# FFN of layer 0: who normalises the rows, and where VectorE takes x's block maxima and scales

## What is computed

```python
xn = _layernorm(x, axis=-1)                 # (x - mean) / sqrt(var + 1e-5)

def fp4_quant_dequant(x):                   # blocks of 16 along the last dim
    xb = x.reshape(shape[:-1] + (shape[-1] // 16, 16))
    scale = max(max(abs(xb)) / 6, 1e-12)
    xn = xb / scale
    idx = searchsorted(_MID, abs(xn))       # to the grid 0, .5, 1, 1.5, 2, 3, 4, 6
    return (_GRID[idx] * sign(xn) * scale).reshape(shape)

fp4_linear = lambda x, w: fp4_quant_dequant(x) @ fp4_quant_dequant(w).T
gate, y = fp4_linear(xn, w_gate), fp4_linear(xn, w_up)     # 352 columns each
x = x + attention(xn) + fp4_linear(silu(gate) * y, w_down)
```

## Time and profile before

| | us |
|---|---|
| runs, median (lowest to highest) | 1184.78 (1180.52 to 1185.24) |
| span of the profiled execution | 1181.7 |
| VectorE busy in that span | 847.8 (72%) |
| TensorE busy | 933.6 (79%) |
| ScalarE busy | 608.6 (52%) |
| GpSimd busy | 357.6 (30%) |

### The profile page before, as it was taken

One profiled execution on the slowest core, in us unless ns is written; L12 is line 12 of the kernel. 1 busy time (PEld: TensorE's weight loads), 2 busy tenths in 40 slices (PEclk: granted clock), 3 DMA queues, 4 the chain that ended last, 5 costly groups with the idle time before them and its releaser, 6 DMA issues.

```text
span 1181.7 us, 35415 instructions
## 1 busy us (share of the span) xinstructions
PE 933.6 (79%) x15259; PEld 526.3 (45%) x15259; DVE 847.8 (72%) x1427; ACT 608.6 (52%) x762; POOL 357.6 (30%) x421
## 2 busy tenths in 40 slices
PE   0578777888877877776678778887898988889887
PEld 0356553334334434443344334443555555455543
DVE  6799956677788888888878855556566577566726
ACT  3233331466655655554355455545555665666666
POOL 3333342203213213213030263543233423522230
PEclk9999976699999999998889899979899999999999
DMA  8700052454233333242222141254264254444117
GB/s 149 234 19 18 19 128 55 86 115 110 67 82 101 79 78 101 56 109 77 53 64 44 45 106 41 61 133 106 68 165 129 79 143 123 133 120 102 58 37 207
DMA packets 115598, 109.32 MB, mean 93 GB/s; under 512 B 13745, under 2 KB 108210, under 8 KB 115058
## 3 DMA queue, kind: packets, MB, share of 16 engines
q1 hardware_dynamic: 108370, 95.30, 32.0%
q0 software_dynamic: 7072, 11.76, 3.7%
HBM read 65.28 MB, written 48.51 MB: 96 GB/s over the span
## 4 chain that ended last, share of the span: by engine, by line
PE 41%; DVE 24%; issue 7%; ACT 6%; another core or an unknown queue 3%; POOL 1%; DMA 1%; SPq 0%; ACTq 0%; DVEq 0%; POOLq 0%
DVE a_maxes L1460 14%; PE a_psO L1243 12%; PE a_psS L1222 6%; PE a_psS L1199 5%; ACT a_Pt L1308 4%; PE a_psS L1084 4%; PE a_psM L1176 2%; PE a_psM L1182 2%; PE a_psM L1110 1%; PE a_psM L1261 1%; DVE xn L1495 1%; PE a_psS L1074 1%; DVE a_ON L1556 1%; ACT parts L1285 1%
## 5 line engine op out<-in xcount | busy, mean ns | idle before, releaser
L1460 DVE TENSOR_REDUCE a_maxes<-a_psS 128x2 f32<-128x1024 f32 (+3 forms) x432 | 505.7, 1182 | 213.4 <-PE a_psS L1084 108.8
L1308 ACT ACTIVATE a_Pt<-a_psS 128x1024 f32<-128x1024 f32 (+1 forms) x432 | 418.1, 990 | 249.8 <-PE a_psS L1084 145.6
L1199 PE MATMUL a_psS<-K,Q 60*64 60x512 bf16 (+3 forms) x2048 | 199.6, 367 | 67.5 <-ACT a_Pt L1308 42.3
L1243 PE MATMUL a_psO<-a_Pt,V 128*32 128x512 f32 (+3 forms) x2048 | 231.8, 543 | 2.5 <-ACT a_Pt L1308 2.5
L1222 PE MATMUL a_psS<-Q,K 63*64 63x512 bf16 (+3 forms) x2048 | 187.3, 368 | 39.2 <-DVE a_maxes L1460 36.4
L1084 PE MATMUL a_psS<-dist,alpha_eye 64*64 64x128 bf16 (+1 forms) x5120 | 175.2, 209 | 5.5 <-issue 5.3
L1084 PEld LDWEIGHTS a_psS<-dist,alpha_eye 64*64 64x64 bf16 x5120 | 155.1, 112 | 50.2 <-issue 14.3
L309 POOL TENSOR_TENSOR qkf<-qkf,parts 128x512 f32<-128x512 f32 x32 | 37.0, 1156 | 325.6 <-ACT parts L1285 324.4
L1222 PEld LDWEIGHTS a_psS<-Q,K 63*64 63x64 bf16 x2048 | 63.1, 107 | 162.1 <-DVE a_maxes L1460 81.5
L1199 PEld LDWEIGHTS a_psS<-K,Q 60*64 60x64 bf16 x2048 | 72.6, 112 | 117.3 <-ACT a_Pt L1308 61.5
L1600 POOL DMA_INDIRECT y<-spare,r_sent_id x64 | 61.6, 962 | 123.8 <-DVE a_maxes L1460 56.5
(11 more groups left out here) (236 smaller groups left out, 1264.0 us busy)
## 6 DMA issues: line engine op xcount, KB each, us to landing
stack<-parts SPq DMA_DIRECT2D x192, 128.0 KB
expert_w<-in_expert_w SPq DMA_DIRECT2D x96, 128.5 KB
Q<-stack SPq DMA_DIRECT2D x64, 192.0 KB
K<-stack SPq DMA_DIRECT2D x64, 192.0 KB
xs<-in_c_no_token SPq DMA_DIRECT2D x24, 258.0 KB, 6.3
slots_flat<-xs SPq DMA_DIRECT2D x24, 258.0 KB, 3.9
xnT<-xnT_dram SPq DMA_DIRECT2D x16, 256.0 KB, 2.8
slots_flat<-y SPq DMA_DIRECT2D x16, 256.0 KB, 4.8
```

Source lines behind the costliest of these rows:

```text
L1199: pe.matmul(banks[HEAD_ROWS * hf:HEAD_ROWS * (hf + 1), b, x * w:(x + 1) * w], Q[rows, k % 4, q, at:at + HEAD_ROWS], K[rows, k % 4, q, 0:w] ...
L1243: m = pe.matmul(psO[32 * j:32 * (j + 1), q0:T], V[:, (k - 2) // 2 % 2, kt, r, j, :], Pt[:, (nB.at(k) + unit) % RING, h % 2, x // 2 * w:(x ...
L1308: act.activation(Pt[:, u % RING, :, 0:w], psS[:, place_of["B", u] % BANK_PAIRS, :, 0:w], ACT.Exp).then_inc(p_ready, 1)
L1460: dve.tensor_reduce(maxes[:, k % 2, i, :, heads[0] // 2:heads[0] // 2 + pairs], src, AX, ALU.max, negate=True).then_inc(a_free, 1)
```

## The change

ScalarE gets a stage `nx` with offset 2 between `a5` and `add`: four instructions of 128 columns that add the negated mean, and after a wait four that multiply by 1/sd, since mean and 1/sd are one number per row and tile. GpSimd's `nx` goes. VectorE's mean becomes a negated mean by the factor -0.5. VectorE's `sx` is cut in two: the block maximum alone stays between the products of tiles 1 and 2, and scale, reciprocal and grid come behind the products of tiles 2 and 3. The waits stay with the steps they guard: the maximum waits for the normalised rows, the scale for GpSimd's scaling of the batch before. Batch 1's x stays whole at the head of `sm(0)`. The positions in `project` and `split` are renumbered, so that these stay where they were.

```diff
-def quant_scales(dve, v, am, sc, rs, least, sem, base):
+def quant_largest(dve, v, am, sem):
 
     dve.tensor_reduce(am, v, AX, ALU.max, apply_absolute_value=True).then_inc(sem, 1)
+
+
+def quant_scales(dve, am, sc, rs, least, sem, base):
+
     dve.wait_ge(sem, base + 1)
...
-                    dve.tensor_scalar(n.mean[:], n.mean[:], 0.5, None, ALU.mult).then_inc(bn_step, 1)
+                    dve.tensor_scalar(n.neg_mean[:], n.neg_mean[:], -0.5, None, ALU.mult).then_inc(bn_step, 1)
...
-                def scales(w, b, p):
+                def largest(w, b, p):
                     dve.wait_ge(*((S["normed"], 2 * b + 2) if w == "x" else (S["h_ready"], NT * b + NT)))
+                    quant_largest(dve, blocks(buf[w + "v"][:, p]), buf[w + "am"][:], S[w + "_grid"])
+
+                def grid(w, b, p):
                     if b:
                         dve.wait_ge(S[w + "_q"], b)
-                    quant_scales(dve, blocks(buf[w + "v"][:, p]), buf[w + "am"][:], buf[w + "sc"][:],
-                                 buf[w + "rs"][:], least[:, 0:buf[w + "sc"].shape[1]], S[w + "_grid"], QUANT_STEPS * b)
-
-                def grid(w, b, p):
+                    quant_scales(dve, buf[w + "am"][:], buf[w + "sc"][:], buf[w + "rs"][:],
+                                 least[:, 0:buf[w + "sc"].shape[1]], S[w + "_grid"], QUANT_STEPS * b)
                     quant_grid(dve, buf[w + "v"][:, p], buf[w + "rs"][:], buf[w + "n"][:], buf[w + "u"][:],
                                S[w + "_grid"], QUANT_STEPS * b)
 
-                def sx(b, p):
+                def sx_largest(b, p):
 
                     if b != 1:
-                        scales("x", b, p)
+                        largest("x", b, p)
+
+                def sx_grid(b, p):
+
+                    if b != 1:
                         grid("x", b, p)
...
                 def sm(b, p):
                     if b == 0:
-                        scales("x", 1, 1)
+                        largest("x", 1, 1)
                         grid("x", 1, 1)
                     multiply(b, p, (0, 1))
...
-                run_ffn_steps([(0, sh), (1, sm), (2, sx), (1, sm_rest)])
+                run_ffn_steps([(0, sh), (1, sm), (2, sx_largest), (1, sm_rest), (2, sx_grid)])
...
+                def nx(b, p):
+                    if b == 0:
+                        act.wait_ge(bn_step, STATS)
+                    if b >= 2:
+                        act.wait_ge(S["xn_turned"], b - 1)
+                        act.wait_ge(S["x_grid"], QUANT_STEPS * (b - 1))
+                    xv = buf["xv"][:, p, :].rearrange("p (i d) -> p i d", d=D)
+                    for i in range(NT):
+                        t = b * NT + i
+                        m = act.activation(xv[:, i, :], n.x[:, t, :], ACT.Identity, bias=n.neg_mean[:, t:t + 1])
+                    m.then_inc(S["normed"], 1)
+                    act.wait_ge(S["normed"], 2 * b + 1)
+                    for i in range(NT):
+                        t = b * NT + i
+                        m = act.activation(xv[:, i, :], xv[:, i, :], ACT.Copy, bias=0.0, scale=n.rstd[:, t:t + 1])
+                    m.then_inc(S["normed"], 1)
...
-                run_ffn_steps([(1, a5), (-1, add), (1, a5_rest), (0, a10), (2, a1_rest)], project)
+                run_ffn_steps([(1, a5), (2, nx), (-1, add), (1, a5_rest), (0, a10), (2, a1_rest)], project)
...
-                    tiles = slice(b * NT, (b + 1) * NT)
-                    xv = buf["xv"][:, p, :].rearrange("p (i d) -> p i d", d=D)
-                    pool.tensor_tensor(xv, n.x[:, tiles, :], bc(n.mean[:, tiles], D), ALU.subtract).then_inc(S["normed"], 1)
-                    pool.wait_ge(S["normed"], 2 * b + 1)
-                    pool.tensor_tensor(xv, xv, bc(n.rstd[:, tiles], D), ALU.mult).then_inc(S["normed"], 1)
...
-                run_ffn_steps([(2, nx), (0, scale_h), (2, scale_x)], split)
+                run_ffn_steps([(0, scale_h), (2, scale_x)], split)
```

More of the change, by code:

```diff
@@ L258, in allocate_constants @@
     n.row_id = n.sb("row_id", [P, 2, TILES], I32)
-    n.mean = n.sb("mean", [P, TILES])
+    n.neg_mean = n.sb("neg_mean", [P, TILES])
     n.rstd = n.sb("rstd", [P, TILES])
@@ L498, in statistics @@
                     dve.wait_ge(bn_step, v)
-                    dve.tensor_tensor(n.mean[:], st[:, :, 1], st[:, :, 4], ALU.add).then_inc(bn_step, 1)
+                    dve.tensor_tensor(n.neg_mean[:], st[:, :, 1], st[:, :, 4], ALU.add).then_inc(bn_step, 1)
                     dve.tensor_tensor(dm[:], st[:, :, 1], st[:, :, 4], ALU.subtract).then_inc(bn_step, 1)
@@ L511, in statistics @@
                     dve.reciprocal(n.rstd[:], sd[:]).then_inc(bn_step, 1)
-                def scales(w, b, p):
+                def largest(w, b, p):
                     dve.wait_ge(*((S["normed"], 2 * b + 2) if w == "x" else (S["h_ready"], NT * b + NT)))
+                    quant_largest(dve, blocks(buf[w + "v"][:, p]), buf[w + "am"][:], S[w + "_grid"])
+                def grid(w, b, p):
                     if b:
                         dve.wait_ge(S[w + "_q"], b)
-                    quant_scales(dve, blocks(buf[w + "v"][:, p]), buf[w + "am"][:], buf[w + "sc"][:],
-                                 buf[w + "rs"][:], least[:, 0:buf[w + "sc"].shape[1]], S[w + "_grid"], QUANT_STEPS * b)
-                def grid(w, b, p):
+                    quant_scales(dve, buf[w + "am"][:], buf[w + "sc"][:], buf[w + "rs"][:],
+                                 least[:, 0:buf[w + "sc"].shape[1]], S[w + "_grid"], QUANT_STEPS * b)
                     quant_grid(dve, buf[w + "v"][:, p], buf[w + "rs"][:], buf[w + "n"][:], buf[w + "u"][:],
                                S[w + "_grid"], QUANT_STEPS * b)
-                def sx(b, p):
+                def sx_largest(b, p):
                     if b != 1:
-                        scales("x", b, p)
+                        largest("x", b, p)
+                def sx_grid(b, p):
+                    if b != 1:
                         grid("x", b, p)
                 def sh(b, p):
-                    scales("h", b, p)
+                    largest("h", b, p)
                     grid("h", b, p)
@@ L559, in _ @@
                 dve.wait_ge(w_loaded, 16 * 7)
-                quant_scales(dve, blocks(w), w_am, w_sc, w_rs, least[:, 0:W // BLK], w_gridded, 0)
+                quant_largest(dve, blocks(w), w_am, w_gridded)
+                quant_scales(dve, w_am, w_sc, w_rs, least[:, 0:W // BLK], w_gridded, 0)
                 quant_grid(dve, w, w_rs, wt, wu, w_gridded, 0)
@@ L606, in project @@
                 def project(it, at):
-                    if it != SEQS - 2 or at not in (0, 2, 3):
+                    if it != SEQS - 2 or at not in (0, 3, 4):
                         return
-                    which = (0, 2, 3).index(at)
+                    which = (0, 3, 4).index(at)
                     act.wait_ge(n.misc_ready, which + 1)
@@ L691, in split @@
                 def split(it, at):
-                    s = {(SEQS - 2, 2): 0, (SEQS - 1, 1): 1}.get((it, at))
+                    s = {(SEQS - 2, 1): 0, (SEQS - 1, 0): 1}.get((it, at))
                     if s is not None:
```

## The result

The kernel after takes 1199.81 us (median of four runs, 1196.89 to 1204.31), the kernel before beside it 1182.65. The ratio is 1.0145, with a 95% interval of 1.0109 to 1.018: slower by 1.1 to 1.8%, or 17.2 us by the medians. The execution profiled has a span of 1195.1 us and is the shortest of the four, so its spans show 13.4 us of the loss.

A forecast was written before the change was run, and what follows sets the result against it. VectorE was taken to set the pace of the middle passes, part of its busy time being waits for GpSimd. Terms 10.1 + 2.8 - 0.5 + 4 x 0.05 - 0.5 = +12.1 us on 1184.78 gave about 1197, range 1190 to 1203.

The forecast's parts named there:

- start, to H0: FFN start: batch 1's normalisation queues behind batch 0's silus, then half-clock gates; first h maximum +10.1 us.
- pass 1: Pass after the first h maximum: half-clock gates of batch 1 no longer covered by x's quantisation; +2.8 us.
- pass 2: Pass of 62.43: two VectorE waits for TensorE go, ScalarE's normalisation ends late; 16.0 instead of 16.47, -0.5 us.
- passes 3 to 6: Four middle passes: 1.6 us of holds return as silu waits; 15.8 us each against 15.76, 4 x 0.05 in all.
- pass 7: Pass of 141.92, without x to quantise: TensorE comes with a little more in hand; -0.5 us.
- last stretch: End of the FFN: 25.44 us set by TensorE's chain, expected to stay.
- The holds: VectorE's scale instruction held by GpSimd: five holds on h, four on x, 6.9 us together, all to go.
- The price of the normalisation: On ScalarE: eight instructions spaced 0.29 us, 2.56 us in all against 2 x 1.04 on GpSimd.
- the clock rival: First two passes: TensorE at full clock for tiles 2 and 3, 2.3 us back each, total +7.5; chance 0.13.
- Middle passes not re-filled: Six passes: gates and silus of tiles 2 and 3 are covered, each keeps 1.6 us, total +2.5; chance 0.07.
- Only the freed port counts: Start hidden as well, so the 6.9 us of holds are net gain: 1177.9 us; chance 0.04.
- Table loads: ScalarE, between silus 1 and 2: two loads of 1.28 us in some eight passes, some +20 more; chance 0.04.

The follow-up runs named there:

- nx_early_old_order: Kernel after with the normalisation a step earlier, behind h's three copies, and VectorE in the order of before; ratio 1.0021 to the kernel before.
- early_old_fill: Kernel after with the normalisation behind h's copies, VectorE's order of before, and four idle transposes behind each part of turned h; 1181.53 us, ratio 0.9961.
- scalar_only: Kernel after with VectorE's order of before, the normalisation still on ScalarE; 1199.06 us, ratio 1.012 to the kernel before.
- fill_h: Kernel after with four idle transposes behind each of the three parts of turned h; 1196.83 us, ratio 1.0112 to the kernel before.
- nx1_ahead: Kernel after with ScalarE normalising batches 0 and 1 before its loop; ratio 1.0029 to the kernel before.
- fill_start: Kernel after with 48 and 40 idle transposes in front of the gates of tiles 2 and 3 of batches 0 and 1; ratio 1.0133 to the kernel before.
- nx_early: Kernel after with the normalisation a step earlier, behind h's three copies where ScalarE is idle; ratio 1.0038 to the kernel before.
- order_only: Kernel after with the normalisation back on GpSimd, leaving VectorE's new order alone; ratio 1.0018 to the kernel before.
- before_fill: Kernel before with four idle transposes behind each part of turned h and nothing else; 1179.70 us, ratio 0.9964.

## Why the prediction was right, and where its sum was off

The forecast was about 1197 us, slower, within 1190 to 1203; 1199.81 came. Term by term, in the order in which the prediction summed them, all from the starts of the h maximum:

| term | forecast | measured | what it was |
|---|---|---|---|
| start, to H0 | +10.1 | +8.8 | 56.02 - 47.24 |
| pass 1 | +2.8 | +2.3 | 17.52 - 15.19 |
| pass 2 | -0.5 | -0.6 | 15.83 - 16.47 |
| passes 3 to 6 | +0.2 | +5.4 | 68.44 - 63.02 |
| pass 7 | -0.5 | +0.9 | 15.39 - 14.51 |
| last stretch | 0 | -1.2 | 24.22 - 25.44, granted clock 0.79 for 0.66 |
| end of the FFN | +12.1 | +15.55 | |

**The holds.** Right for the nine that were counted. "All go" left out the tenth, by a GpSimd instruction for the attention, which stays (1.03 us at 174.92) and was no part of the sum. The Trainium skill (SBUF — State Buffer, on the pair of ports that VectorE and GpSimd share) has the loser blocked for the whole of the other's instruction; the traces agree with it in both directions, with 0.25 and 0.18 us where GpSimd is quiet, and 1.00 to 1.16 where the scaling of h runs (nx_early_old_order, early_old_fill).

**The price of the normalisation.** Right: 45.33 - 42.77 = 2.56 us to the end of the last instruction, the forecast's own figure, with the spacing of about 0.29 that was taken from the earlier trace rows. No table load was added.

**The start.** Right in mechanism, 1.3 too much in size. I put the end of silu 1 at 44.4; it was 42.87, mostly because TensorE ran the second pair of gates faster (ScalarE waited 0.96 for it, 1.88 before). That part is luck of this execution: in scalar_only and fill_h, with the same start, the wait was 1.88 again and the first product came at 49.98 and 50.50, against the forecast 50.8. From there to the first product it took 6.4 us as forecast, and from that to H0 6.7 for the 6.5 forecast, at half clock as forecast. nx1_ahead shows that the queue place is the cause, and fill_start that the half clock was worth the 2.3 us that the clock rival gave it (6.72 - 4.29 = 2.4; the 6.72 was 6.1 and 6.0 in scalar_only and fill_h).

**The middle passes: the term that was mis-sized.** "So the 1.6 us of holds come back as 1.6 us of waits for silu, and I cost a middle pass at nothing." The first half is right to the tenth where nothing else interferes: in nx_early h takes 8.52 us (forecast 8.5), tile 0's product to tile 3's 4.26 (4.3), the rest of x 3.13 (3.2), together 15.83 (15.8), and the waits are 1.67. Pass 2 of the kernel after is the same 15.83. From the third pass on the kernel after pays 1.3 us more, four times over: h 8.60, products 115.20 to 120.63 = 5.43, x 3.12. The step took TensorE at full clock, as the middle pass of the earlier trace rows had it. One pass of before did have slow output groups:

```profile
94.64:110.43 15.79, 13.27 (x68) 10.20 (x68) 14.45 (x19) 4.91 (x11) 5.69 (x5) 0.89 0.05 18
```

```profile
94.92 1.52 PE L751 MATMUL f_ps_d<-wdT,f_hqT 128*128 128x128 f32 x6 [0.68 <-ACT f_hqT L604]
...
106.31 0.19 DVE L327 SCALAR_TENSOR_TENSOR f_xsc<-f_xam,f_least 128x32 f32<-128x32 f32 x1
```

It was no longer than the others, because VectorE had its holds in hand: x's scale, late itself, met no hold there (0.19 for 1.22). The change used up that slack, and put the normalisation right behind the silu that a slow TensorE delays: silu 1 came 1.5 us later, the normalisation with it, and behind that the maximum, the output copy and silus 2 and 3. It takes both: fill_h takes away the slow groups and leaves the place (15.83); nx_early takes away the place, and the one middle pass that has the slow groups is 15.92; order_only has VectorE's new order and slow groups in one pass without the place, and they cost nothing there. By the prediction's own signs, middle passes over 17 were to speak against it, and 17.06 to 17.23 came.

**Pass 7.** No x is left to normalise there, so the place has no part in it; TensorE's slow groups alone lengthen it. It takes 15.39 after and 15.48 in order_only, both at a granted clock of 0.90, and 13.92 in fill_h and nx_early at 1.00, which is the -0.5 that the forecast gave it.

**What was right by cancelling.** The forecast was 1.3 too high at the start, 0.5 in pass 1 and 1.2 in the last stretch, and too low by 5.2 in passes 3 to 6 and by 1.4 in pass 7. The range held the time because its upper end reckoned with a dip of the clock that the old order would have absorbed, though as one dip and not as one in each pass. The time also came out nearer than the loss: 17.2 us by the medians against the 12.1 of the sum, but added to a median of before that was 2.1 lower (1182.65 of four runs, where the forecast started from 1184.78 of three).

**The rivals.** Clock stays up: no, the gates behind both pauses ran slow. Middle passes not re-filled: no, order_only and nx_early show the 1.67 us of waits. Only the freed port counts: no; freeing it gained 0.5 us a pass, and that only with the normalisation in the idle slot and TensorE at full clock (early_old_fill, and every other pass of nx_early_old_order). Table loads: none came. The Trainium skill (Perfetto Trace Analysis, Optimizing Scalar/DVE Operations) says that offloading some work to ScalarE may make sense if VectorE is saturated. In this case the work came off GpSimd, and the runs agree for that slot alone (15.27 us a pass in early_old_fill for 15.75 in before_fill).

## What to carry to other kernels

Whether it pays to move an instruction to an idler engine was decided here by its place in that engine's queue, not by the engine's load: the same 2.6 us cost some 15 us of the FFN behind silu 1, and nothing behind the copies. When a change takes the slack out of the pace-setting engine, look for what that slack was hiding, here a pass of before in which TensorE had run slow at no cost. And where TensorE waits often and briefly, look at the granted clock by pass and at the length of equal groups before blaming the new work.

## What the runs showed that I had not expected

The slow stretch can lock to the pass. In the kernel after it falls on the same two output groups (1.65 and 1.49 us) in every pass from the third to the sixth, in nx_early_old_order on every other pass, and in nx_early, which makes the same TensorE instructions in the same order, on one of the passes 2 to 6 (1.65 and 1.43 from 126.34 on). What fixes the place was not found; it came also after three waits of only 0.69 us (before 89.06 in the kernel after). From the next pass on the first of the three is 1.69, because the copy stands behind the late silus; whether that keeps the slow stretch in its place was not tested.

Idle transposes can make a kernel faster. Twelve a pass, on an engine that is busy 13.27 of 17.07 us, made a pass 1.2 us shorter (fill_h), and in the last stretch of before they gave 2.7 us (granted clock 0.92 for 0.66). Where the pace is set elsewhere they give nothing: 15.75 against 15.76 us in the middle passes of before.
